# Three residual additions of a gated two-layer block moved from VectorE into TensorE's accumulation, copied out by ScalarE

## The reference, cut to what matters

```python
x = x + tanh(g_xattn[0]) * attention(layernorm(x), ctx, ...)          # 16 heads, rotary
x = x + tanh(g_ffn[0])   * experts(layernorm(x), Wr, W1, b1, W2, b2)  # 8 experts, top 2 per sequence, GELU
x = x + tanh(g_xattn[1]) * autocorrelation(layernorm(x), ctx, ...)    # lags found through a Fourier transform
x = x + tanh(g_ffn[1])   * mlp(layernorm(x), w_gate, w_up, w_down)    # 352 hidden, FP4 rounding of inputs, hidden values and weights
```

## Time and profile before

| | |
|---|---|
| device time, three runs | 307.54, 307.99 (median), 312.88 us |
| device time of the profiled execution | 307.39 us |
| its span, first to last instruction | 305.6 us |
| TensorE busy | 265.2 us, 87% |
| VectorE busy | 202.5 us, 66% |
| ScalarE busy | 158.4 us, 52% |
| GpSimd busy | 115.2 us, 38% |
| mean granted TensorE clock | 0.966 of full speed |

### The profile page before, as it was taken

The page is one execution under the profiler, slowest core; times in us unless marked ns, Lnnn a source line. Parts: engine busy times, 40 slices in busy tenths (PEclk is TensorE's granted clock), DMA queues, the critical chain, the costliest instruction groups (busy, mean ns, idle before and its releaser), DMA issues.

```text
span 305.6 us, 6321 instructions
## 1 busy us (share of the span) xinstructions
PE 265.2 (87%) x2208; PEld 206.2 (67%) x2208; DVE 202.5 (66%) x545; ACT 158.4 (52%) x361; POOL 115.2 (38%) x168
## 2 busy tenths in 40 slices
PE   1999999999899988999999987996885959696965
PEld 1555467666668778999999965874753636474855
DVE  3499988888987722532223269544279799999881
ACT  1269365666587468755666645315524624343421
POOL 4274459993202132199722015200334331313121
PEclk9999999999999999999999997999998877887999
DMA  7995000000000286776777300000000000010001
GB/s 239 361 383 221 0 3 2 2 2 2 0 3 2 77 328 247 282 319 276 286 303 304 151 0 3 0 2 0 1 0 2 1 0 0 0 30 23 17 17 55
DMA packets 11871, 30.15 MB, mean 99 GB/s; under 512 B 960, under 2 KB 5056, under 8 KB 11712
## 3 DMA queue, kind: packets, MB, share of 16 engines
q1 hardware_dynamic: 11840, 29.75, 25.7%
HBM read 9.75 MB, written 1.05 MB: 35 GB/s over the span
## 4 chain that ended last, share of the span: by engine, by line
PE 59%; DVE 24%; ACT 7%; issue 6%; POOL 2%; DMA 2%; SPq 0%; DVEq 0%; ACTq 0%; POOLq 0%
PE ps L1266 11%; PE ps L1255 10%; PE ps L1116 5%; PE ps L1090 4%; PE ps L1439 4%; PE ps L1103 4%; DVE s_region L278 4%; DVE s_region L684 3%; DVE s_small L227 2%; PE ps L1325 2%; PE ps L1303 2%; PE ps L1126 2%; PE ps L1378 2%; DMA s_ctxT<-ctxT 2%; DVE s_region L691 1%
## 5 line engine op out<-in xcount | busy, mean ns | idle before, releaser
L551 ACT ACTIVATE s_region<-ps,s_region 128x128 f32<-128x128 f32 x144 | 41.0, 372 | 20.3 <-PE ps L1255 20.2
L838 DVE SCALAR_TENSOR_TENSOR s_ctxT<-ps,s_region,s_ctxT 128x64 f32 x72 | 18.2, 281 | 49.2 <-PE ps L1266 48.6
L1266 PE MATMUL ps<-s_region 128*128 128x128 f32 x288 | 38.1, 276 | 1.3 <-ACT s_region L551 1.3
L1255 PE MATMUL ps<-s_region 128*128 128x128 f32 x288 | 38.0, 276 | 0.1
L1266 PEld LDWEIGHTS ps<-s_region 128*128 128x128 f32 x288 | 35.0, 192 | 1.7 <-ACT s_region L551 1.5
L250 POOL TENSOR_TENSOR s_small<-s_small,s_par 128x4 f32<-128x4 f32 (+3 forms) x14 | 15.5, 1108 | 53.3 <-DVE s_small L233 53.3
L1255 PEld LDWEIGHTS ps<-s_region 128*128 128x128 f32 x288 | 34.9, 192 | 0.3 <-issue 0.2
L285 POOL TENSOR_TENSOR s_region<-s_region,s_small 128x704 f32<-128x704 f32 (+2 forms) x13 | 17.5, 1344 | 44.8 <-DVE s_region L278 44.8
L1439 PE MATMUL ps<-s_region 128*128 128x352 f32 x64 | 26.4, 569 | 2.3 <-ACT s_region L621 2.3
L384 POOL COPY s_region<-s_xt 128x64 f32 x72 | 14.9, 242 | 34.0 <-PE ps L1255 23.8
L498 ACT COPY s_region<-ps 128x512 f32<-128x512 f32 x32 | 17.2, 589 | 18.2 <-PE ps L1103 18.2
(11 more groups left out here) (207 smaller groups left out, 509.7 us busy)
## 6 DMA issues: line engine op xcount, KB each, us to landing
s_region<-s_wall SPq DMA_DIRECT2D x36, 514.0 KB, 3.1
s_wall<-wall SPq DMA_DIRECT2D x8, 514.0 KB, 9.2
s_par<-par SPq DMA_DIRECT2D x1, 1316.0 KB, 10.9
s_ctxT<-ctxT SPq DMA_DIRECT2D x2, 512.0 KB, 6.1
s_x<-x SPq DMA_DIRECT2D x2, 512.0 KB, 7.4
out<-s_x SPq DMA_DIRECT2D x8, 128.0 KB, 1.8
s_region<-ffn SPq DMA_DIRECT2D x1, 560.0 KB, 3.6
s_par<-par SPq DMA_DIRECT2D x1, 460.0 KB, 4.0
```

Source lines behind the costliest of these rows:

```text
L551: ins = act.activation(hg[j % 3][:, c, :], ps[:, j % 3, RPT * S * c:RPT * S * (c + 1)], ACT.Gelu, bias=wbuf[j % 6][:, FF + FC * D + c:FF + ...
L1255: ins = mm(ps[:, j % 3, RPT * S * c:RPT * S * (c + 1)], w[:, P * c:P * c + P], xg[j % 4], start=True, stop=True)
L1266: ins = mm(ps[:, 4 + j % 2, 0:RPT * S], w[:, FF + D * c:FF + D * c + D], hg[j % 3][:, c, :], start=(c == 0), stop=(c == FC - 1))
```

## The change

- **Experts.** `turn_experts` becomes `add_experts`. TensorE first writes `identity x x` of the group (512 columns) into the bank and leaves the accumulation open. Instead of a transpose by the identity, the four tiles of `acc` are then multiplied by `identg`, the identity times the gate, into the same bank. The sum is complete in PSUM. ScalarE copies it to `x` in `experts_added`; VectorE keeps only the statistics. `identg` is one new VectorE instruction.
- **Second attention.** `out_tokens` first puts `identity x x` of the group into the bank and adds its product to it; banks 5 and 6 alternate. The gate is applied when ScalarE copies bank 4 into `y1` (an activation with a scale instead of a copy). ScalarE's new `attention_added` copies the sum to `x`.
- **MLP.** `down` first puts `identity x x` of the pair (256 columns) into bank 7. The gate goes into the down weights when `weights_turned(2)` copies them. `finish` moves from VectorE to ScalarE as a copy, in front of the copy into `hT`.
- Waits follow: POOL's last `normalise` waits for `x2_done`, VectorE's `bias_added` too.

```diff
+            def experts_added(g):
+                act.wait_ge(m["x2_tr"], g + 1)
+                act.copy(x[:, 4 * g:4 * g + 4, :].rearrange("p t d -> p (t d)"), ps[:, 4 + g % 2, :]).then_inc(m["x2_done"], 1)
+            def attention_added(g):
+                act.wait_ge(m["o_done"], g + 1)
+                act.copy(x[:, 4 * g:4 * g + 4, :].rearrange("p t d -> p (t d)"), ps[:, 5 + g % 2, :]).then_inc(m["x3_done"], 1)
...
             def y1_turned(g):
                 act.wait_ge(m["y1_done"], g + 1)
-                act.copy(y1.rearrange("p a b -> p (a b)"), ps[:, 4, :]).then_inc(m["y1_ready"], 1)
+                act.activation(y1.rearrange("p a b -> p (a b)"), ps[:, 4, :], ACT.Identity, scale=tg[:, 2:3]).then_inc(m["y1_ready"], 1)
 
             kv_turned(2)
+            experts_added(0)
             kv_turned(3)
-            for g in range(3):
-                normalise(act, 4 * g, 4 * g + 4, m["xn_c"], 7 + g)
-                x_turned(g)
+            experts_added(1)
+            normalise(act, 0, 4, m["xn_c"], 7)
+            experts_added(2)
+            x_turned(0)
+            experts_added(3)
+            normalise(act, 4, 8, m["xn_c"], 8)
+            x_turned(1)
+            normalise(act, 8, 12, m["xn_c"], 9)
+            x_turned(2)
             x_turned(3)
...
+            attention_added(0)
             normalise(act, 0, 4, m["xn_d"], 11)
             y1_turned(2)
+            attention_added(1)
             normalise(act, 4, 8, m["xn_d"], 12)
             x_magnitude(0)
             y1_turned(3)
+            attention_added(2)
+            attention_added(3)
             turned_x(0)
...
+            def finish(q):
+                act.wait_ge(m["dn_done"], q + 1)
+                act.copy(x[:, 2 * q:2 * q + 2, :].rearrange("p t d -> p (t d)"), ps[:, 7, 0:2 * D]).then_inc(m["x4_done"], 1)
+
+            for q in range(PAIRS + 2):
...
+                if q >= 2:
+                    finish(q - 2)
+                if 1 <= q <= PAIRS:
                     act.wait_ge(m["ht_done"], q)
...
+            dve.tensor_scalar(identg, pc("ident"), tg[:, 1:2], None, ALU.mult).then_inc(m["ident_scaled"], 1)
...
-                dve.wait_ge(m["x2_tr"], g + 1)
-                dve.scalar_tensor_tensor(group(x, g), ps[:, 4 + g % 2, :], tg[:, 1:2], group(x, g),
-                                         ALU.mult, ALU.add).then_inc(m["x2_done"], 1)
...
-                dve.scalar_tensor_tensor(group(x, g), ps[:, 5, :], tg[:, 2:3], group(x, g), ALU.mult, ALU.add).then_inc(m["x3_done"], 1)
...
-                dve.scalar_tensor_tensor(both, ps[:, 7, 0:2 * D], tg[:, 3:4], both, ALU.mult, ALU.add).then_inc(m["x4_done"], 1)
...
+            def add_experts(g):
+
+                if g < 2:
+                    pe.wait_ge(m["acc_done"], SLOTS - RPT * (1 - g))
+                else:
+                    pe.wait_ge(m["x2_done"], g - 1)
+                mm(ps[:, 4 + g % 2, :], ident, x[:, 4 * g:4 * g + 4, :].rearrange("p t d -> p (t d)"), start=True, stop=False)
                 pe.wait_ge(m["acc_done"], SLOTS)
-                if g >= 2:
-                    pe.wait_ge(m["x2_done"], g - 1)
                 for k in range(4):
-                    ins = tr(ps[:, 4 + g % 2, P * k:P * k + P], acc[:, 8 * g + 2 * k:8 * g + 2 * k + 2, :].rearrange("p b s -> p (b s)"), ident)
+                    ins = mm(ps[:, 4 + g % 2, P * k:P * k + P], acc[:, 8 * g + 2 * k:8 * g + 2 * k + 2, :].rearrange("p b s -> p (b s)"), identg,
+                             start=False, stop=(k == 3))
...
             def out_tokens(g):
+                pe.wait_ge(m["bo_added"], g + 1)
+                if g == 0:
+                    pe.wait_ge(m["gx_ready"], 2)
+                if g >= 2:
+                    pe.wait_ge(m["x3_done"], g - 1)
+                bank = 5 + g % 2
+                mm(ps[:, bank, :], ident, x[:, 4 * g:4 * g + 4, :].rearrange("p t d -> p (t d)"), start=True, stop=False)
                 pe.wait_ge(m["y1_ready"], g + 1)
-                if g:
-                    pe.wait_ge(m["x3_done"], g)
-                mm(ps[:, 5, :], pc("idft_o"), y1.rearrange("p a b -> p (a b)"), start=True, stop=True).then_inc(m["o_done"], 1)
+                mm(ps[:, bank, :], pc("idft_o"), y1.rearrange("p a b -> p (a b)"), start=False, stop=True).then_inc(m["o_done"], 1)
...
+                mm(ps[:, 7, 0:2 * D], ident, x[:, 2 * q:2 * q + 2, :].rearrange("p t d -> p (t d)"), start=True, stop=False)
```

More of the change, by code:

```diff
@@ L111, in build @@
         region = sb("region", [28480])
-        small = sb("small", [2136])
+        small = sb("small", [2264])
         ps = ctx.enter_context(nc.psum_tensor("ps", [P, 8, 512], F32))
@@ L197, in build @@
         bo1g = sm(D)
+        identg = sm(P)
         wmx, wsc, win = sm(NB_W), sm(NB_W), sm(NB_W)
@@ L202, in build @@
         hmx = [sm(2 * NH, 2)[:, :, 0] for _ in range(3)]
-        assert taken[0] <= 2136, taken[0]
+        assert taken[0] <= 2264, taken[0]
         names = """ld_par ld_x0 ld_x1 ld_ctx0 ld_ctx1 ld_rest ld_ctxn ld_wall ld_ffn kbd_first kbd_second kbd_done spare_zero vbd_zero vbd_half hmask_ready bias_rows bias_product bias_ready x_biased gates preloaded
@@ L211, in build @@
         w0 w1 w2 w3 w4 w5 xg_done h_done hg_done y2_done acc_done
-        wsc_ready wabs_ready wv_ready wm_ready wq_ready wq_tr wq_used bo_scaled bo_added
+        wsc_ready wabs_ready wv_ready wm_ready wq_ready wq_tr wq_used bo_scaled bo_added ident_scaled x2_read x3_read
         x2_tr x2_done xn_c xn_c_late xf_done xf_used q_done pp_done hs_done hs_read hs_turned cf_ready corr_done corr_read
@@ L407, in _ @@
                 powers(pool, 4 * g, 4 * g + 4)
+            pool.wait_ge(m["x2_done"], G4)
             normalise(pool, 12, 16, m["xn_c_late"], 10)
@@ L565, in weights_turned @@
                 dst = wdT.rearrange("p c d -> p (c d)") if g == 2 else wguT[:, MT * P * g:MT * P * (g + 1)]
-                act.copy(dst, ps[:, 2 + g % 2, 0:MT * P]).then_inc(m["wq_used"], 1)
+                src = ps[:, 2 + g % 2, 0:MT * P]
+                ins = act.activation(dst, src, ACT.Identity, scale=tg[:, 3:4]) if g == 2 else act.copy(dst, src)
+                ins.then_inc(m["wq_used"], 1)
+            def experts_added(g):
[4 more added lines that the diff above has]
+                act.copy(x[:, 4 * g:4 * g + 4, :].rearrange("p t d -> p (t d)"), ps[:, 5 + g % 2, :]).then_inc(m["x3_done"], 1)
             def x_turned(g):
@@ L649, in _ @@
             normalise(act, 12, 16, m["xn_d"], 14)
-            for q in range(PAIRS + 1):
+            def finish(q):
+                act.wait_ge(m["dn_done"], q + 1)
+                act.copy(x[:, 2 * q:2 * q + 2, :].rearrange("p t d -> p (t d)"), ps[:, 7, 0:2 * D]).then_inc(m["x4_done"], 1)
+            for q in range(PAIRS + 2):
                 if q + 1 < PAIRS:
@@ L912, in bias_added @@
                 dve.wait_ge(m["bo_scaled"], 1)
+                dve.wait_ge(m["x2_done"], g + 1)
                 dve.wait_ge(*((m["xn_c_late"], 4) if g == 3 else (m["xn_c"], 4 * g + 4)))
@@ L934, in _, with out_and_stats @@
             dd = Steps(dve, m["dve_d"])
[L936 to L941 removed]
+            def out_and_stats(g):
                 dve.wait_ge(m["x3_done"], g + 1)
@@ L975, in pair_step @@
                     k = dd.mark(dve.tensor_reduce(hmx[n3], blocks(flat), AX, ALU.max, apply_absolute_value=True))
-                if q >= 3:
-                    finish(q - 3)
                 if first:
@@ L982, in pair_step @@
                     fp4_shrunk(dve, blocks(flat), blocks(flat), spread(hin[n3], 2 * NH)).then_inc(m["hv_done"], 1)
-            def finish(q):
-                dve.wait_ge(m["dn_done"], q + 1)
-                both = x[:, 2 * q:2 * q + 2, :].rearrange("p t d -> p (t d)")
-                dve.scalar_tensor_tensor(both, ps[:, 7, 0:2 * D], tg[:, 3:4], both, ALU.mult, ALU.add).then_inc(m["x4_done"], 1)
-            def out_and_stats(g):
-                attention_out(g)
-                x_stats(g)
             out_and_stats(0)
@@ L1003, in _ @@
             x_scale(1)
-            for q in range(PAIRS + 3):
+            for q in range(PAIRS + 1):
                 pair_step(q)
@@ L1344, in _ @@
             context_kv(2)
-            turn_experts(0)
-            turn_experts(1)
+            add_experts(0)
+            add_experts(1)
             context_kv(3)
-            turn_experts(2)
-            turn_experts(3)
+            add_experts(2)
+            add_experts(3)
             to_frequency(0)
@@ L1462, in down @@
                         n = min(P, MLP - P * k)
-                        ins = mm(ps[:, 7, D * t:D * t + D], hT[q % 2][0:n, t, k, :], wdT[0:n, k, :], start=(k == 0), stop=(k == MT - 1))
+                        ins = mm(ps[:, 7, D * t:D * t + D], hT[q % 2][0:n, t, k, :], wdT[0:n, k, :],
+                             start=False, stop=(t == 1 and k == MT - 1))
                 ins.then_inc(m["dn_done"], 1)
```

6 lines of the change are left out of this document (removed).

## The result

The changed kernel takes 316.55 us (median of four runs: 316.49, 318.03, 316.6, 313.79) where the kernel before takes 307.97 on the same chip. The ratio is 1.027, 95% interval 1.020 to 1.034: slower. The forecast was 314.8 us, range 310.6 to 317.2.

What follows compares the result with a forecast made beforehand. TensorE was taken as the first bound (59% of the chain), VectorE the second (24%), with limits of their own at the three places. 307.39 + 1.1 (experts) + 6.3 (second attention) + 0 (MLP) = 314.8 us, range 310.6 to 317.2.

Steps and rivals of the forecast that it cites:

- Second attention, +6.3: End of the second attention: sum copies wait behind the next group's `y1` copy, TensorE idles, its clock falls; +6.3 us.
- The rival in which the clock does not fall: Second attention: the clock stays full or is back at once, +3.9 instead of +6.3, total 312.4 us; 17%.
- Its mark, a pause under about 2 us: Second attention: the rival without a clock fall decides from where TensorE's pause is under about 2 us.
- Experts, +1.1: End of the experts: identity products and ScalarE copies delay the statistics by 1.06 and `sum_heads(0)` to 194.3; +1.1 us.
- its lower bound: End of the experts: 0 if the transforms catch up, since TensorE ran at a lower clock there before.
- MLP, 0: MLP: eight additions of 0.48 leave VectorE but gain 0, since L980 ends with POOL's L285 anyway.
- The end, taken as even: End of the MLP: uncovered identity product (+0.43) against VectorE waits saved, taken as even within 0.5 us.
- The fuller TensorE keeps its clock in the MLP: MLP: extra `down` work avoids a lower-clock spell, saving 3.4 us; total 311.4, or 309.4 with L987's 2.0; 15%.
- The other two rivals: VectorE's count decides: 297.6 us if all on the path, 3%; ScalarE's list binds the MLP too: 321.4 us, 7%.

Runs made afterwards that it cites:

- Experiment 2: The changed kernel with ScalarE's list reordered in the second attention: each sum's copy goes ahead of the next group's `y1` activation; ratio 1.003 to the kernel before.
- experiment 3: The changed kernel with 20 unread products of 128 columns filling TensorE's pause ahead of `out_product(3)`; ratio 1.021 to the kernel before.
- experiment 6: The experts' part alone on the kernel before, with `to_frequency(0)` ahead of `add_experts(3)` and the second normalisation ahead of `experts_added(3)`; ratio 1.011.
- experiment 4: POOL scales back only half the hidden values, in the kernel before (305.3 us) and in that kernel with the MLP part alone (306.4 us).
- best: Kernel before plus reordered attention part and MLP part, identity product ahead of the wait for `hT`, experts' addition on VectorE; ratio 0.988 to the kernel before.
- best_again: The same kernel as `best`, unchanged, on another chip job; ratio 0.989 to the kernel before.
- all_ordered: `best` with the experts' part added in its better order, so all three additions on TensorE and ScalarE; ratio 1.001 to the kernel before.
- mlp_alone: The kernel before with only the MLP's part of the change; ratio 0.999 to the kernel before.
- best_fill: `best` with eight more unread TensorE products around 110 us, four in the routing and four in the experts' first slot; ratio 0.991 to the kernel before.

## Why the prediction was right, and what it missed

- **Second attention, +6.3: +5.94.** Right in each link. Less the 3.78 us that had come in ahead (2.42 + 0.06 + 1.30), `out_product(1)` starts at 223.86 and `attention_added(0)` ends at 226.12 in the clock of the profile before; 223.86 and 226.26 were forecast. VectorE's L935 follows at 227.62, 2.1 late (forecast 2.2), and group 1's statistics at 232.89 instead of 227.63, 5.26 late (forecast 5.55). VectorE idle 3.86 (forecast 4), TensorE's pause 5.01 (forecast 5.4), clock 0.50, back 5.0 us after `out_product(3)` began (3.4 to 6.8). The activation with a scale takes 0.69 (0.72 taken). Experiment 2 shows the cause, experiment 3 the two prices. The rival in which the clock does not fall gave +3.9 at this place; with the clock held full it is +3.7. Its mark, a pause under about 2 us, does not hold: the fall at 235.0 in the kernel before comes behind a pause of 1.95 (233.32 in the earlier trace rows).
- The Trainium skill, "TensorE: Matmul & The Clock Gate", section "HAM oscillation — how this bites in real kernels", was taken as a warning against such a pause: the trace agrees, at 2.2 us. The larger part is the wait itself, 5.0 us at full clock, of which no clock rule speaks.
- **Experts, +1.1: +1.30.** The statistics were 1.19 late (1.06). The working gave the kernel after at full clock, link by link, and named the lower clock of the kernel before only in its lower bound. So the net came out right, and the price of the part itself, 2.8 us at one clock (experiment 6), was not seen; 0.8 of it is list position.
- **MLP, 0: −0.72**, and 0 in every pair that runs at full clock. L980 ends with POOL's operation with and without the addition, and experiment 4 frees it. No semaphore of POOL stands ahead of L980, so the sentence at the start that the engines wait for each other only through semaphores is too strong. The Trainium skill, "GPSIMD Engine Reference", section "8. Key points", names contention for two SBUF inputs or a 2-port mode: the trace agrees in that POOL is the cause (0.68 and 0.41, 0.18 with POOL's operation halved), while which of the two conditions L980 meets no run here tells. The end, taken as even, is: 13.73 and 13.71.
- **The fuller TensorE keeps its clock in the MLP** (15%) is not refuted as a smaller effect. Lengthened pairs add 0 us in four of the eight profiled kernels of full length with the MLP part, 0.3 and 0.5 in `best` and `best_again`, 1.1 in the kernel after and 1.8 in `all_ordered`; in the four without it they add 1.2 to 2.3. That is 1.2 us less in the mean, less than the 3.4 of the rival. But `mlp_alone` as a whole gives 0.999 with 0.8% either way, so 1.2 us can be neither shown nor excluded by run times. The other two rivals did not come: taking sixteen additions off VectorE shortened no stretch that was compared at one clock, and with `finish` in front of the `hT` copy no pair got longer.
- **What was missed: +2.4 us ahead of the experts.** It alone is more than the 1.6 us by which the difference of the spans exceeds the forecast, and than the 1.75 by which the median does. Windows at this place, of the kernel after, then of the MLP part alone:

```profile
110.00:112.00 2.00, 2.00 (x9) 0.70 0.93 376
...
116.00:118.00 2.00, 2.00 (x13) 0.60 0.65 267
```

```profile
110.00:112.00 2.00, 2.00 (x9) 0.72 0.96 387
116.00:118.00 2.00, 2.00 (x13) 0.58 0.65 265
```

TensorE is busy for both windows and runs at the lower clock in code that none of these edits touch, behind a wait of 1.05 us (108.69 to 109.75). The kernel before has this wait too, and no fall. What differs lies at the start of the execution, some 90 us before the first edited instruction: the first sixteen 64-wide products of TensorE, before and after.

```profile
9.83 1.09 PE L1035 MATMUL ps<-s_par,s_ctxT 128*64 128x128 f32 x16
```

```profile
9.64 1.98 PE L1047 MATMUL ps<-s_par,s_ctxT 128*64 128x128 f32 x16
```

In five of the fourteen profiles these take 1.09 to 1.25 us, and none of the five has the fall at 110; in nine they take 1.71 to 1.98, since TensorE is still at half speed in them (in the kernel after two 512-column products take 2.05 us at 5.96 and 1.02 at 12.62), and eight of these have it. The ninth is `best_fill`, which fills the place. `best` (1.97) and `best_again` (1.09) are the same instructions, with 114.15 and 111.25 us to the first `hidden`. So the +2.4 us is a thing of the execution, set before the changed code is reached: 0.9 is there at 103 us, the rest comes with the fall. How often an execution of either kernel starts late, the few profiles do not tell.
- The sum was of terms for one execution, while the clock's placement moves a run by more than the smaller terms. That the total came out near the forecast is owed to the attention term: without the +2.4 of the start and the −0.72 of the clock in the MLP the spans differ by 7.3, where 7.4 was forecast. That it came out over 2% is owed in part to the start; the fastest of the four runs, 313.79, is 1.9% over the kernel before.

## What to carry to other kernels

Taking an addition off a busy engine pays only if the copy that replaces it gets its turn when the sum is ready. Read the in-order list of the engine that takes it: what stands ahead, and what that waits for. Work out what each stage waits for before counting saved operations, since the eight of the MLP were worth nothing here while GpSimd held the next instruction. Put an identity product ahead of the wait that the real product has. And compare a stretch only with one at the same clock: the experts' part looked like 1.3 us and costs 2.8.

## What the runs showed of the hardware

- Stretches at the lower clock move between executions of one kernel, and the time goes with them: runs of the kernel before took 306.31 us at a mean granted clock of 0.970, 308.05 at 0.967 and 310.54 at 0.956. Whether one lies at 110 us went, in thirteen of fourteen profiles, with whether TensorE reached full speed early or late at the start.
- A 44-column operation of VectorE that reads and writes local memory (L980) waits for the end of POOL's 704-column operation: 0.68, 0.41 and 0.18 us. The maximum (0.88 beside POOL's operation, 0.89 without) does not, nor does the addition that reads PSUM (0.47 to 0.48). The reciprocal starts only when POOL's operation has ended, so the runs do not tell. It is not so beside every operation of POOL: the 32-column L268 takes 0.18 us beside POOL's L250 (229.82 in the kernel before) and 0.18 alone.
- An activation of 512 columns from PSUM with a per-partition scale takes 0.69 us, the copy 0.58 to 0.59.
